# Local attention blocks: the second half's inverse deviation by GpSimd's power and a Newton step, Gelu's table loaded behind the first square root

## What is computed

```python
def _layer(x, wqkv, qs, ksc, wo, lg, lb, w1, b1, w2, b2):
    ...                                   # local attention, giving o
    x = x + o @ wo
    h = shift_token(x)                    # channels 64..127 come from the token before
    mu = h.mean(-1, keepdims=True)
    var = h.var(-1, keepdims=True)
    h = (h - mu) / jnp.sqrt(var + 1e-05) * lg + lb
    h = h @ w1 + b1
    a, g = jnp.split(h, 2, axis=-1)
    h = a * jax.nn.gelu(g, approximate=False)
    x = x + h @ w2 + b2
    return x
for l in range(DEPTH):                    # DEPTH = 2
    x = _layer(x, ...)
```

## Time and profile before

| | us |
|---|---|
| median of 3 runs | 4165.23 |
| lowest, highest | 4162.58, 4172.28 |
| the profiled execution's own time | 4182.44 |
| its span in the trace | 4180.5 |
| granted TensorE clock, mean | 0.941 of full speed |

### The profile page before, as it was taken

The page is one execution under the profiler, slowest core; times in us unless marked ns, Lnnn a source line. Parts: engine busy times, 40 slices in busy tenths (PEclk is TensorE's granted clock), DMA queues, the critical chain, the costliest instruction groups (busy, mean ns, idle before and its releaser), DMA issues. The chain is left out here.

```text
span 4180.5 us, 79738 instructions
## 1 busy us (share of the span) xinstructions
PE 3646.5 (87%) x29896; PEld 2052.8 (49%) x29896; DVE 2644.4 (63%) x5977; ACT 2156.3 (52%) x4999; POOL 867.3 (21%) x1071
## 2 busy tenths in 40 slices
PE   5988978888989996799899999989888998888987
PEld 3656654444545453333333343345555665555565
DVE  5667646565555654777777777647565665664766
ACT  3555544544555554365565665654554554454454
POOL 1111001000010001223233142135212331431421
PEclk8999988989988998799999999999999999999999
DMA  3221211111101101101111011012120230321212
GB/s 108 61 51 37 71 30 47 41 29 24 44 18 44 29 13 64 50 20 48 29 43 34 23 39 34 13 41 62 36 74 23 62 82 8 81 61 28 55 42 55
DMA packets 149543, 183.52 MB, mean 44 GB/s; under 512 B 34568, under 2 KB 102216, under 8 KB 145832
## 3 DMA queue, kind: packets, MB, share of 16 engines
q1 hardware_dynamic: 143268, 171.01, 15.5%
q10 hardware_dynamic: 5892, 7.41, 0.7%
HBM read 91.69 MB, written 34.08 MB: 30 GB/s over the span
## 5 line engine op out<-in xcount | busy, mean ns | idle before, releaser
L1375 ACT ACTIVATE prob<-ps_st 128x512 f32<-128x512 f32 (+3 forms) x2432 | 1124.3, 510 | 1110.9 <-PE ps_st L1312 589.5
L1408 DVE TENSOR_REDUCE mhalf<-mx 128x1 f32<-128x512 f32 (+3 forms) x2064 | 1254.4, 652 | 575.2 <-PE mx L1349 319.1
L1346 PE MATMUL mx<-ks,qs 56*128 56x512 bf16 (+4 forms) x2304 | 629.9, 367 | 137.7 <-DVE g_tok L1983 52.5
L1283 PE MATMUL ps_st<-qs,ks 59*128 59x512 bf16 (+4 forms) x2432 | 624.4, 352 | 50.6 <-ACT prob L1375 36.2
L1269 PE MATMUL ps_o<-prob,vst 128*32 128x256 f32 (+3 forms) x6512 | 596.6, 447 | 0.8 <-ACT prob L1375 0.4
L1283 PEld LDWEIGHTS ps_st<-qs,ks 75*128 75x128 bf16 (+1 forms) x2432 | 192.0, 97 | 407.9 <-ACT prob L1375 275.7
L1346 PEld LDWEIGHTS mx<-ks,qs 72*128 72x128 bf16 (+1 forms) x2304 | 192.6, 100 | 402.9 <-DVE mhalf L1408 76.1
L1458 POOL COPY vst<-v_tok 128x256 f32<-128x256 f32 x48 | 19.9, 418 | 1158.4 <-PE ps_o L1269 1141.7
L3337 ACT ACTIVATE o<-ps,nm,lrq 128x128 f32<-128x128 f32 x512 | 227.1, 461 | 51.3 <-DVE nm L3454 24.7
L1269 PEld LDWEIGHTS ps_o<-prob,vst 128*32 128x32 f32 x6512 | 136.9, 110 | 223.1 <-issue 124.9
L1290 PE MATMUL ps_st<-qx,kx 64*128 64x512 bf16 x1024 | 210.6, 390 | 0.0
(11 more groups left out here) (483 smaller groups left out, 6560.1 us busy)
## 6 DMA issues: line engine op xcount, KB each, us to landing
qs<-q_scr SPq DMA_DIRECT2D x186, 96.0 KB
ks<-k_scr SPq DMA_DIRECT2D x90, 192.0 KB
lkt<-o SPq DMA_DIRECT2D x256, 64.0 KB, 2.0
lve<-lv SPq DMA_DIRECT2D x24, 512.0 KB, 4.8
lqt<-o SPq DMA_DIRECT2D x160, 64.0 KB, 2.0
tabs<-local_tables SPq DMA_DIRECT2D x4, 2048.0 KB, 7.7
k_scr<-part SPq DMA_DIRECT2D x30, 256.0 KB, 3.1
lqt<-o ACTq DMA_DIRECT2D x96, 64.0 KB, 2.1
```

The source lines that it names most:

```text
L1283: return nc.tensor.matmul(score_bank(GH * b + n)[:, 0:q1 - q0], ks[g % 2][row:row + R + 3, lane, kt * P:(kt + 1) * P], qs[g % 2][row:row + ...
L1346: last = nc.tensor.matmul(bank[:, j * w:(j + 1) * w], qs[g % 2][row:row + R, hf, lane, (t - 4 * hf) * P:(t - 4 * hf + 1) * P], ks[g % 2][r ...
L1375: nc.scalar.activation(prob[:, b % PROBS, h, 0:q1 - q0], ps_st[:, u % 3, 0:q1 - q0], ACT.Exp, scale=scale).then_inc(S["exped"], 1)
L1408: nc.vector.tensor_reduce(mhalf[:, hf, h0:h0 + heads, t - 4 * hf, part], bank[:, 0:heads * (k1 - k0)].rearrange("p (n w) -> p n w", n=head ...
```

## The change

Per local block, the second half's root no longer goes through ACT. DVE writes variance plus epsilon into `std` as before; POOL raises it to the power -0.5 into `rstd` (128x4 elements, exponents from a tile `minus` filled earlier by a memset); DVE refines that by one Newton step of three instructions, r' = (1.5 - 0.5 v r²) r, and goes on with the four `tensor_scalar`. On POOL the power stands ahead of the second bias addition. ACT loses `deviations(1)` and issues `load_table` for Gelu right behind `deviations(0)`. There are two more semaphores and two small tiles.

```diff
@@ names of the phase's semaphores
-                                 ... "stat", "var", "spread", "std", "rstd", ...
+                                 ... "stat", "var", "spread", "std", "minus", "power", "rstd", ...
@@ tiles
+            near = net.tmp("near", [P, 4])
+            minus = net.tmp("minus", [P, 4])
@@ ACT
                     deviations(0)
+                    load_table(net, 4, ACT.Gelu)
                     units_ch(0)
-                    deviations(1)
                     act.wait_ge(S["mm"], NT)
@@ DVE, to_units(i)
                         ts = slice(4 * i, 4 * i + 4)
-                        dve.wait_ge(S["std"], i + 1)
-                        nc.vector.reciprocal(rstd[:, ts], std[:, ts]).then_inc(S["rstd"], 1)
+                        if i == 0:
+                            dve.wait_ge(S["std"], 1)
+                            nc.vector.reciprocal(rstd[:, ts], std[:, ts]).then_inc(S["rstd"], 1)
+                        else:
+                            dve.wait_ge(S["power"], 1)
+                            nc.vector.tensor_tensor(near[:, :], rstd[:, ts], rstd[:, ts], ALU.mult).then_inc(S["power"], 1)
+                            dve.wait_ge(S["power"], 2)
+                            nc.vector.scalar_tensor_tensor(out=near[:, :], in0=near[:, :], scalar=-0.5, in1=std[:, ts], op0=ALU.mult,
+                                                           op1=ALU.mult).then_inc(S["power"], 1)
+                            dve.wait_ge(S["power"], 3)
+                            nc.vector.scalar_tensor_tensor(out=rstd[:, ts], in0=near[:, :], scalar=1.5, in1=rstd[:, ts], op0=ALU.add,
+                                                           op1=ALU.mult).then_inc(S["rstd"], 1)
                         dve.wait_ge(S["rstd"], i + 1)
@@ POOL
                     pool.wait_ge(S["sums"], NT - 1)
+                    nc.gpsimd.memset(minus[:, :], -0.5).then_inc(S["minus"], 1)
                     nc.gpsimd.memset(late[0:1, 0, HC:C], 0.0).then_inc(S["first"], 1)
@@ POOL, for i in range(2)
                         pool.wait_ge(*((S["sent"], 32), (S["shifted"], 2))[i])
                         ts = slice(4 * i, 4 * i + 4)
+                        if i == 1:
+                            pool.wait_ge(S["minus"], 1)
+                            pool.wait_ge(S["spread"], 2)
+                            nc.gpsimd.tensor_tensor(rstd[:, ts], std[:, ts], minus[:, :], ALU.pow).then_inc(S["power"], 1)
                         nc.gpsimd.tensor_tensor(net.xn_tok[:, ts, :], net.xn_tok[:, ts, :],
                                                 W(f"l3_b2{d}").unsqueeze(1).broadcast_to([P, 4, C]), ALU.add).then_inc(S["biased"], 1)
@@ build
-        net.unread = net.sbuf("unread", [P, 4])
+        net.unread = net.sbuf("unread", [P, 5])
```

More of the change, by code:

```diff
@@ L2986, in local_block @@
                                  "s", "raw", "max", "exped", "tp", "copied", "o", "inv", "norm", "turned", "ch", "mm", "sum", "low", "first", "sent",
-                                 "shifted", "high", "stat", "var", "spread", "std", "rstd", "unit", "unit_t", "in_ch", "hid", "gelu", "gated",
+                                 "shifted", "high", "stat", "var", "spread", "std", "minus", "power", "rstd", "unit", "unit_t", "in_ch", "hid", "gelu", "gated",
                                  "biased", "outp", "new"]) as (S, blk):
```

## The result

| | before | after |
|---|---|---|
| median us | 4170.66 (11 runs) | 4190.99 (11 runs) |
| lowest, highest | 4162.58, 4187.85 | 4172.45, 4216.23 |
| the profiled execution's own time | 4182.44 | 4172.45 |

A forecast was written before the change was run, and what follows sets the result against it. It took PE, waiting in each tail for DVE's first gated product, as the bound. Four d=0 and four d=1 tails, 4 (0.45 - 0.28) + 4 (0.45 - 0.09) = +2.1 us, gave 4167.3 us, range 4157 to 4190.

The forecast's parts named there:

- `spreads(1)` held by POOL's addition, and freed by the change: Second half's small DVE instruction in each tail: 0.17 us instead of 1.09, as POOL would be idle when it starts.
- ACT leaves the path to G: Tail: Gelu's table load hides behind the first root at no cost; the first Gelu ends two us earlier, near 4032.45.
- G: Start of DVE's first gated product in a tail, which releases `into(2)` on PE; 4034.45 in the last d=0 tail before.
- The power's price, 0.45 us: POOL, between `spreads(1)` and its second addition: 0.19 us plus 4 x 0.063, from 30 additions an element; bounds 0.14 to 1.27.
- 8d - 1.5: The slow-power rival's formula for the whole kernel's time change in us, over eight tails; no change up to d = 1.2.
- d: Duration of one 128x4 power on POOL, taken as 0.45 us.
- The Newton step held by POOL's addition: DVE in the tail: first Newton instruction ends with POOL's addition; G moves d - 0.28 (d=0) or d - 0.09 us (d=1) later.
- The end of a tail moves by as much as G: PE's chain behind `into(2)` in each tail: fixed order without slack, so any shift of G passes unchanged to the end.
- The rival "slow power": POOL between `spreads(1)` and its second addition: slower from d = 1.2 us on, +22.5 us at d = 3; chance 0.25.
- The rival "doesn't do what it says": ACT in the tail: early table load has no effect, load ends at 4030.77, same time as forecast; no chance of its own.

The follow-up runs named there:

- the reordering alone: Kernel before, with only POOL's second bias addition made to wait for DVE's eight units; roots stay on ACT, no power: 4160.44 us, ratio 0.9984 [0.9964, 1.0005].
- the kernel with its gap filled: Changed kernel plus nine dummy matmuls on TensorE between `into(1)` and `into(2)`: 4176.24 us, ratio 1.0020 [1.0002, 1.0038] to the kernel before.

## Why the prediction was wrong, step by step

- *`spreads(1)` held by POOL's addition, and freed by the change:* right, 0.17 us in all eight tails; the reordering alone shows that it was POOL.
- *ACT leaves the path to G:* right. The load fits behind the first root, as costed: in the last d=0 tail of the trace after, `in_ch` still waits 0.39 us for PE behind the dummy activation (0.45 in the d=1 tail shown).
- *The power's price, 0.45 us:* wrong, it is 1.02. It lay inside the bounds (0.14 to 1.27) but far from the value taken. The fixed part was right (0.20, from additions 0.19), with some luck: it mixed a mean of 727 ns with POOL's longest addition, and with the shortest (1089) the same sum gives 0.37. No run shows the 30 additions an element that it took; the runs show 0.82 us beyond the fixed part, as much as some 100. By the forecast's own formula, 8d - 1.5 with d = 1.02 is +6.7 us; the eight shifts of G sum to 6.5, and with the clock kept up the runs show +8 (1 to 16). This term was short by 4.4 us.
- *The Newton step held by POOL's addition:* right; the shift of G comes out to 0.02 us in either kind of tail. G was forecast at d - 0.28 and d - 0.09 later, 0.74 and 0.93 with the true d, and came 0.73 and 0.91 later. Part of that is luck: POOL started its power 0.17 to 0.18 us behind `spreads(1)`, not 0.06 (it has three waits to go through there, perhaps for that), and G started 0.08 us before the units' last row ends (4143.73 against 4142.70 + 1.11), not 0.03 behind it; the two offset each other. The Trainium skill's page SBUF — State Buffer ("Who interferes with whom") has the rule as these runs show it: an exclusive lock for a whole instruction, here 1.05 to 1.24 us for 0.16 us of work.
- *"The end of a tail moves by as much as G":* this is the step that failed. It holds in half of the tails of the trace after (0.7 and 0.9 us) and in every tail of the kernel with its gap filled. In the others a lower clock adds 1.6 to 2.9 us, 9.0 in all. The prediction had the gap of PE before its eyes (1.78 us: clock 1.00), lengthened it by its own sum, and took PE at full clock behind it for any d. At its own d = 0.45 the gaps would have been 1.8 to 1.95 us, and no run shows what the clock does there; at the 2.3 to 2.5 that came it had no term. The trace of before had the warning, though in another part of the block, where PE waits for a DMA for 2.59 us:

```profile
4113.69 0.59 PE L3182 MATMUL ps<-local_qk_bf,ident_bf 128*128 128x512 bf16 x2 [2.59 <-DMA lkt<-o]
```

```profile
4105.00:4111.10 6.10, 4.94 (x82) 3.47 (x79) 5.25 (x13) 4.94 (x21) 0.00 (x0) 1.00 0.34 80
4111.10:4113.69 2.59, 0.00 (x1) 0.03 (x1) 1.25 (x4) 1.07 (x6) 0.00 (x0) 1.00 0.32 76
4114.50:4117.50 3.00, 3.00 (x51) 2.55 (x44) 0.00 (x0) 0.00 (x0) 0.00 (x0) 0.50 0.00 0
```

The clock is 1.00 up to the gap and 0.50 less than a microsecond behind it. That, and a helper called `keep_clock` in the kernel's own text, were reason for a rival, and there was none.

- *How the sum fails, then:* forecast +2.1 us; 4.4 more for the power and 9.0 for the clock make 15.5 in the one trace, where the runs show +20 (12 to 28). The other 5 were not located; the trace is of the changed kernel's fastest run, and others may have had more tails at the half clock.
- *The rival "slow power"* had the place right and set the point where it decides at d = 1.2 us. Since it too left the clock out, it was reached at 1.02.
- *The rival "doesn't do what it says":* it put an automatically placed load behind `units_ch(0)`, at 4029.49. It stands behind the next wait instead, the one for the first hidden product (4031.75 in that tail), 2.3 us later. For the changed kernel the conclusion (no effect) still holds, as the run without the load shows; its reason was wrong.

## What to carry to other kernels

Before moving a small operation to GpSimd, price it there by one product of the same shape and one of the real function; a 128x4 power costs 1.02 us, a product 0.20. A long POOL instruction set right behind one for which VectorE waits mostly takes the port first (here 32 of 32 times behind a power, 7 of 8 behind a product), so give it a wait that lets VectorE through: with that one line and the table load behind the second root, and no power, the tails of this kernel got 5.3 us shorter and its runs 0.33% faster, where the change lost 0.47%. And when an edit lengthens a gap of TensorE, look at the granted clock behind it: the gap may cost more after its end than in it, and dummy matmuls in it are a quick test.

## What the runs showed of the hardware that was not expected

- TensorE's clock in these tails: with an idle stretch of at most 1.78 us ahead of `into(2)` none of 56 tails was lengthened (seven kernels: the one before, and those with gap filled, reordered, or with a product). With 2.32 to 2.52 us, 9 of 16 were (the changed kernel and the one without the early load), by 1.4 to 2.9 us each. With 3.30 to 3.50 us, 8 of 8. Nothing was run between 1.78 and 2.32.
- These counts hold for this place. The same gap need not do the same each time, and elsewhere a shorter one goes before a fall: in the trace of before the clock is 0.50 from 3858.60 on, and PE's longest idle stretch in the 8 us before that is 1.42 us.

```profile
3857.50 5.75 PE L253 MATMUL ph<-ident_bf 128*128 128x512 bf16 x18 [1.42 <-DVE st L2234]
```

```profile
3858.60:3861.80 3.20, 3.20 (x9) 1.18 (x8) 1.77 (x8) 1.91 (x6) 0.00 (x0) 0.50 0.00 0
```

- The scatter of this program goes with that clock. The changed kernel's fastest run (4172.45 us) had a mean granted clock of 0.947, its slowest (4216.23) 0.934. Its range of 44 us against 25 for the kernel before says less than it seems, since 35 further runs of the kernel before range over 39 us.
- A 128x4 power on GpSimd costs 1.02 us, 0.82 more than a product of the same shape, the same at the first use and the second.
- A table load that is placed automatically waits with the instruction that it serves (0.34 us behind the root in the reordered kernel, released by PE); the one of an explicit dummy activation started at once (0.02 us behind the root).
